# A fused attention, mixture of experts and recurrence kernel: two of four result tables read while the last experts run, and the last-slot store on another queue

## What is computed

```python
x = x + attention(layernorm(x))       # 16 heads of 16, 4 key groups, causal, soft cap
x = x + ffn(layernorm(x))
x = x + recurrence(layernorm(x))      # gates, then a scan over the rows
x = x + ffn(layernorm(x))

def ffn(x):                            # 64 experts, each row to 6 of them, 96 slots per expert
    topk_w, topk_i = top_k(masked softmax(x @ gate.T), 6)
    slot = expert * 96 + min(position among the expert's rows, 95)
    buf  = zeros(64 * 96, 256).at[slot].set(x[row])
    out  = (silu(buf @ Wg.T) * (buf @ Wu.T)) @ Wd.T       # per expert
    y    = sum over the 6 of out[slot] * topk_w
    return y + shared expert(x)
```

## Time and profile before

| | us |
|---|---|
| median of 3 runs | 1242.32 |
| the profiled execution's own time | 1246.5 |
| its span in the trace | 1244.3 |
| TensorE busy | 992.2 (80%) |
| ScalarE busy | 739.2 (59%) |
| DVE busy | 520.0 (42%) |
| POOL busy | 409.6 (33%) |
| attention, with the first routing of three and a half chunks | 0 to 600 |
| last half chunk, store of the last slots | 600 to 660 |
| experts, f = 0 | 660 to 821 |
| results, recurrence, second routing | 821 to 1050 |
| experts, f = 1 | 1050 to 1210 |
| results and stores | 1210 to 1244 |

### The profile page before, as it was taken

How to read it: one execution, slowest core, us unless ns; L and a number is a source line. 1 busy time by engine, 2 the same in 40 slices (tenths; PEclk the granted TensorE clock), 3 DMA queues, 4 the chain that set the end, 5 groups by cost and what they waited for, 6 DMA issues and landing times.

```text
span 1244.3 us, 20310 instructions
## 1 busy us (share of the span) xinstructions
PE 992.2 (80%) x7268; PEld 641.1 (52%) x7268; DVE 520.0 (42%) x1575; ACT 739.2 (59%) x982; POOL 409.6 (33%) x404
## 2 busy tenths in 40 slices
PE   5888787887888888877717999945787674999978
PEld 3543233332345455444316999932444443999966
DVE  7772711454212342430522333347876740333325
ACT  3588999999999999999102444414453300444420
POOL 0000000001230034055122556620288884566550
PEclk9999888988999999999667999966799876999987
DMA  9991000000110012000686999648132524999948
GB/s 352 394 392 69 1 1 1 18 1 17 49 55 29 1 49 74 10 14 3 196 221 172 289 290 288 144 135 267 62 125 108 174 56 116 267 296 283 264 56 329
DMA packets 94948, 176.21 MB, mean 142 GB/s; under 512 B 13134, under 2 KB 46895, under 8 KB 94848
## 3 DMA queue, kind: packets, MB, share of 16 engines
q1 hardware_dynamic: 57904, 130.02, 31.3%
q0 software_dynamic: 23616, 28.44, 10.8%
q10 hardware_dynamic: 13328, 16.45, 4.8%
HBM read 107.30 MB, written 83.72 MB: 154 GB/s over the span
## 4 chain that ended last, share of the span: by engine, by line
PE 28%; POOL 10%; DMA 4%; SPq 3%; issue 3%; DVE 2%; DVEq 1%; ACT 0%; POOLq 0%; ACTq 0%
PE PS L1465 14%; PE PS L1476 9%; POOL expert_in L335 7%; POOL pause L343 2%; PE PS L1452 2%; SPq L1261 2%; SPq L1262 1%; PE PS L1521 1%; PE PS L1505 1%; DMA expert_in<-lrow 1%; DMA spare_space<-expert_out 1%; DMA XE<-expert_in 1%; PE PS L1554 1%; DMA expert_out<-ob,yidx 1%; POOL expert_out L1351 0%
## 5 line engine op out<-in xcount | busy, mean ns | idle before, releaser
L335 POOL DMA_INDIRECT expert_in<-xp,didx x192 | 192.8, 1004 | 617.9 <-ACT PR L779 495.1
L774 ACT ACTIVATE PR<-PS 128x1024 f32<-128x1024 f32 (+3 forms) x312 | 277.1, 963 | 29.2 <-PE PS L643 13.7
L779 ACT ACTIVATE PR<-PR 128x2048 f32<-128x2048 f32 (+3 forms) x156 | 274.5, 1762 | 0.0
L1351 POOL DMA_INDIRECT expert_out<-ob,yidx x128 | 180.6, 1411 | 168.7 <-ACT ob L1663 125.8
L663 PE MATMUL PS<-PR,V 128*32 128x512 f32 (+3 forms) x768 | 96.0, 574 | 41.0 <-ACT PR L779 40.8
L1910 DVE SCALAR_TENSOR_TENSOR gta<-gth,PS 88x192 f32<-88x192 f32 x128 | 44.8, 350 | 193.1 <-ACT gth L1653 193.1
L643 PE MATMUL PS<-QT,KT 96*128 96x512 bf16 (+3 forms) x384 | 104.0, 364 | 12.2 <-ACT PR L774 9.4
L1653 ACT ACTIVATE gth<-PS 88x192 f32<-88x192 f32 x128 | 41.9, 327 | 107.1 <-PE PS L1465 107.1
L1663 ACT ACTIVATE ob<-PS,wslot 96x256 f32<-96x256 f32 x128 | 60.2, 470 | 61.8 <-PE PS L1476 59.5
L1465 PEld LDWEIGHTS PS<-XT,spare_space 128*88 128x88 f32 x960 | 92.0, 163 | 8.8 <-issue 2.6
L1465 PE MATMUL PS<-XT,spare_space 128*88 128x96 f32 x960 | 93.1, 253 | 2.1 <-ACT XT L1644 1.1
(11 more groups left out here) (271 smaller groups left out, 1535.0 us busy)
## 6 DMA issues: line engine op xcount, KB each, us to landing
spare_space<-in_wgu SPq DMA_DIRECT2D x60, 352.0 KB
expert_out<-zero SPq DMA_DIRECT2D x2, 8256.0 KB, 51.0
expert_in<-zero SPq DMA_DIRECT2D x2, 7776.0 KB, 39.6
XE<-expert_in ACTq DMA_DIRECT2D x32, 486.0 KB, 9.9
WGU<-in_wgu SPq DMA_DIRECT2D x44, 352.0 KB
spare_space<-expert_out SPq DMA_DIRECT2D x24, 512.0 KB, 6.2
spare_space<-in_wd SPq DMA_DIRECT2D x60, 176.0 KB
shared_space<-in_wgu SPq DMA_DIRECT2D x24, 352.0 KB
```

The lines of the kernel that those rows point to most:

```text
L335: pool.indirect_dma_start(out=buf_d[f], out_offset=bass.IndirectOffsetOnAxis(ap=didx[b][:, r, j:j + 1], axis=0), in_=xp[b][:, r, :], in_of ...
L774: act.activation(PR[:, n % 3, 2 * pr:2 * pr + 2, cols(v, s):CW], PS[:, S0 + 2 * pr:S0 + 2 * pr + 2, cols(v, s):CW], ACT.Tanh, scale=1.0 / ...
L779: act.activation(PR[:, n % 3, :, lo:CW], PR[:, n % 3, :, lo:CW], ACT.Exp, scale=SOFT_CAP).then_inc(exp_done, 1)
L1351: pool.indirect_dma_start(out=y_d[f], out_offset=bass.IndirectOffsetOnAxis(ap=yidx[:, n % 4, j:j + 1], axis=0), in_=ob[:, i % EU, :], in_o ...
```

## The change

- The store of the last slots is issued by ScalarE, which waits for the gathered rows itself, ahead of its waits for the dispatches.
- Experts 0 to 47 use the four tables as before. Experts 48 to 51 use tables 0, 1, 2, 0, and from 52 on only tables 0 and 1 in turn. `send(e)` waits for the expert that used its table last: 52 for 51, 54 for 52, and so on two apart.
- SP reads all of table 3 (when expert 47's rows have landed and its `down` is done) and all of table 2 (after expert 50's) as one DMA each, 16 rows of 1 KB to a partition, into two parts of `spare_space` whose weights have been used by then.
- DVE adds them to X, a chunk at a time: table 3 behind its products for experts 54 to 57, table 2 behind those for 59 to 62. The reads of the results also wait for these eight additions.
- After the experts two tables are read, 2 KB to a partition of a tile, and DVE and TensorE add two instead of four.
- `add_results(2)` moves behind `recur_inputs(0)`.

Cut to its core; `add_results`, the tiles by DVE in `combine_late`, the buffers `late_results` and the index table of `slot_meta` change in the same way, and f = 1 as f = 0:

```diff
--- before.py
+++ after.py
 NACC = 4
+LATE = 2
+TABLE_GROUPS = (0, 12, 13)
+
+def table_of(e):
+    return e % 4 if e < 48 else (e - 48) % 3 if e < 52 else e % 2
+
+def last_in_table(e, j):
+    return max([i for i in range(e) if table_of(i) == j], default=None)
...
-    ybase = np.broadcast_to(YBIG + np.arange(EH)[None, :] % NACC, (P, EH))
+    ybase = np.broadcast_to(YBIG + np.concatenate([tables[EH * h:EH * (h + 1)] for h in TABLE_GROUPS])[None, :], (P, EH * len(TABLE_GROUPS)))
...
-        GB = place_at(0, NACC).rearrange("p (r n) -> p r n", r=CT)
+        TA, TB = (place_at(NACC * i, NACC).rearrange("p (i n) -> p i n", i=NT) for i in range(2))
+        GB = place_at(0, LATE).rearrange("p (r n) -> p r n", r=CT)
...
-            def last_slots(f):
-                sp.wait_ge(last_rows, 16 * (f + 1))
-                sp.dma_start(buf_d[f].rearrange("(e s) c -> e s c", s=CAP)[:, CAP - 1, :], lrow[:]).then_inc(last_stored, 16)
...
+            def retired_tables(f):
+                for j, space, user in ((3, TA, 47), (2, TB, 50)):
+                    last = f * E + last_in_table(E, j)
+                    sp.wait_ge(y_sent[last % EU], 16 * (last // EU + 1))
+                    sp.wait_ge(down_psum, f * E + user + 1)
+                    sp.dma_start(space, y_d[f][0:NACC * T, :].rearrange("(i p k) c -> p i k c", p=P, k=NACC)[:, :, j, :]).then_inc(table_ld[3 - j], 16)
...
                         sp.wait_ge(y_sent[q], 16 * (E // EU) * (f + 1))
+                    sp.wait_ge(tables_added, 2 * NC * (f + 1))
                     sp.dma_start(O95[:], y_d[f][NACC * T:YROWS, :]).then_inc(o95_loaded, 16)
...
-                    sp.dma_start(results_tile, y_d[f][NACC * P * i:NACC * P * (i + 1), :].rearrange("(p k) c -> p (k c)", k=NACC))\
+                    sp.dma_start(results_tile.rearrange("p (k c) -> p k c", k=LATE),
+                                 y_d[f][NACC * P * i:NACC * P * (i + 1), :].rearrange("(p k) c -> p k c", k=NACC)[:, 0:LATE, :])\
...
-            last_slots(0)
             experts(0)
+            retired_tables(0)
...
-                if e >= NACC:
-                    pool.wait_ge(y_sent[(i - NACC) % EU], 16 * ((i - NACC) // EU + 1))
+                if last_in_table(e, table_of(e)) is not None:
+                    last = f * E + last_in_table(e, table_of(e))
+                    pool.wait_ge(y_sent[last % EU], 16 * (last // EU + 1))
...
-                        for j in range(NACC):
+                        for j in range(LATE):
                             last = pe.matmul(late_bank(i), const("ident"), late_results[c][:, r, j * C:(j + 1) * C], start=False,
...
+                act.wait_ge(last_rows, 16 * (f + 1))
+                act.dma_start(buf_d[f].rearrange("(e s) c -> e s c", s=CAP)[:, CAP - 1, :], lrow[:]).then_inc(last_stored, 16)
                 for b in range(NXP):
                     act.wait_ge(dispatched[b], 16 * CT * TOPK * chunks_in(b, NC * (f + 1)))
...
                     dve.drain()
+                    for j, space, first in ((0, TA, 54), (1, TB, 59)):
+                        if first <= e < first + NC:
+                            c = e - first
+                            dve.wait_ge(table_ld[j], 16 * (f + 1))
+                            xc = X[:, CT * c:CT * (c + 1), :]
+                            dve.tensor_tensor(xc, xc, space[:, CT * c:CT * (c + 1), :], ALU.add).then_inc(tables_added, 1)
...
-                tables = GB[:, r, :].rearrange("p (j n) -> p j n", j=NACC)
-                dve.tensor_tensor(tables[:, 0:2, :], tables[:, 0:2, :], tables[:, 2:4, :], ALU.add)
-                dve.drain()
-                dve.tensor_tensor(tables[:, 0, :], tables[:, 0, :], tables[:, 1, :], ALU.add)
+                dve.tensor_tensor(GB[:, r, 0:C], GB[:, r, 0:C], GB[:, r, C:2 * C], ALU.add)
...
             statistics(1, None)
-            add_results(2)
             for c in range(NC + 1):
...
                     recur_inputs(c)
+                if c == 0:
+                    add_results(2)
```

More of the change, by code:

```diff
@@ L73, in constants @@
     base = np.broadcast_to(BIG - CAP * e, (P, E))
-    lastv = YBIG - (NACC * T + p[:, None] - p[:, None] % NACC)
+    tables = np.array([table_of(i) for i in range(E)])
+    lastv = YBIG - (NACC * T + p[:, None] - np.resize(tables, P)[:, None])
     ycode = YBIG - NACC * (P * np.arange(NT)[None, :] + p[:, None])
-    ybase = np.broadcast_to(YBIG + np.arange(EH)[None, :] % NACC, (P, EH))
+    ybase = np.broadcast_to(YBIG + np.concatenate([tables[EH * h:EH * (h + 1)] for h in TABLE_GROUPS])[None, :], (P, EH * len(TABLE_GROUPS)))
     tok = P * np.arange(NT)[None, :] + p[:, None] + 1.0
@@ L183, in hybrid_kernel @@
         y_sent = [sem(f"y_sent{i}") for i in range(EU)]
+        table_ld, tables_added = [sem(f"table_loaded{i}") for i in range(2)], sem("tables_added")
         y_ld = [sem(f"y_loaded{i}") for i in range(CT)]
@@ L1219, in hybrid_kernel @@
         O95 = keep("O95", [E, C])
-        result_width = CT * NACC * C
+        result_width = CT * LATE * C
         late_results = [GB, WGU[:].rearrange("p e h m -> p (e h m)")[:, 0:result_width].rearrange("p (r n) -> p r n", r=CT),
                         WD_space[:, 0:result_width].rearrange("p (r n) -> p r n", r=CT),
-                        place_at(NACC, NACC).rearrange("p (r n) -> p r n", r=CT)]
+                        place_at(NACC, LATE).rearrange("p (r n) -> p r n", r=CT)]
         hc = keep("hc", [P, CH])
@@ L1316, in _ @@
             first_spare2(1)
-            last_slots(1)
             experts(1)
+            retired_tables(1)
             for c in range(NC):
@@ L1519, in combine_late @@
                         pe.wait_ge(late_ld[c][r], 16)
-                        for j in range(NACC):
+                        for j in range(LATE):
                             last = pe.matmul(late_bank(i), const("ident"), late_results[c][:, r, j * C:(j + 1) * C], start=False,
-                                             stop=(j == NACC - 1), skip_group_check=True)
+                                             stop=(j == LATE - 1), skip_group_check=True)
                     last.then_inc(rows_summed, 1)
@@ L1895, in slot_meta @@
                 w0 = C + EH * h
+                group = sum(h >= h0 for h0 in TABLE_GROUPS) - 1
                 dve.tensor_copy(wslot[:, s, :], flat[:, w0:w0 + (EH - 1) * (RW + 1) + 1:RW + 1])
-                dve.tensor_tensor(yidx[:, s, :], const("ybase")[0:CAP, :], XE[:, h % 2, :, VCOL], ALU.subtract)\
+                dve.tensor_tensor(yidx[:, s, :], const("ybase")[0:CAP, EH * group:EH * (group + 1)], XE[:, h % 2, :, VCOL], ALU.subtract)\
                    .then_inc(meta_ready, 1)
@@ L1926, in combine_late @@
                         dve.wait_ge(late_ld[c][r], 16)
-                        tables = rows[:, r, :].rearrange("p (j q n) -> p j q n", j=NACC // 2, q=2)
-                        dve.tensor_tensor(tables[:, :, 0, :], tables[:, :, 0, :], tables[:, :, 1, :], ALU.add)
-                    dve.drain()
-                    dve.tensor_tensor(rows[:, r0:r1, 0:C], rows[:, r0:r1, 0:C], rows[:, r0:r1, 2 * C:3 * C], ALU.add)
+                        dve.tensor_tensor(rows[:, r, 0:C], rows[:, r, 0:C], rows[:, r, C:2 * C], ALU.add)
                     dve.drain()
@@ L1969, in add_first_tile @@
                 dve.wait_ge(y_ld[r], 16)
-                tables = GB[:, r, :].rearrange("p (j n) -> p j n", j=NACC)
-                dve.tensor_tensor(tables[:, 0:2, :], tables[:, 0:2, :], tables[:, 2:4, :], ALU.add)
+                dve.tensor_tensor(GB[:, r, 0:C], GB[:, r, 0:C], GB[:, r, C:2 * C], ALU.add)
                 dve.drain()
-                dve.tensor_tensor(tables[:, 0, :], tables[:, 0, :], tables[:, 1, :], ALU.add)
-                dve.drain()
-                added = dve.tensor_tensor(X[:, r, :], X[:, r, :], tables[:, 0, :], ALU.add)
+                added = dve.tensor_tensor(X[:, r, :], X[:, r, :], GB[:, r, 0:C], ALU.add)
                 if r == CT - 1:
@@ L1982, in add_results @@
                     dve.wait_ge(y_ld[r], 16 * (c + 1))
-                    tables = GB[:, r, :].rearrange("p (j q n) -> p j q n", j=NACC // 2, q=2)
-                    dve.tensor_tensor(tables[:, :, 0, :], tables[:, :, 0, :], tables[:, :, 1, :], ALU.add)
-                dve.drain()
-                dve.tensor_tensor(GB[:, :, 0:C], GB[:, :, 0:C], GB[:, :, 2 * C:3 * C], ALU.add)
+                dve.tensor_tensor(GB[:, :, 0:C], GB[:, :, 0:C], GB[:, :, C:2 * C], ALU.add)
                 dve.drain()
```

## The result

| | before | after |
|---|---|---|
| median of 8 runs each, us | 1242.26 (1238.23 to 1243.95) | 1250.26 (1246.05 to 1257.96) |
| profiled execution, own time and span | 1246.5, 1244.3 | 1252.13, 1250.3 |
| mean granted clock in it (TensorE) | 0.901 | 0.896 |

**The change is slower: ratio 1.0069 [1.0046, 1.0093], 8.0 us.** Forecast were 1239 us and a range to 1250.

What follows compares the result with a forecast made beforehand. It took a chain of waits to bound the kernel: store and input load, TensorE in the stages, DVE then POOL between, TensorE's tail sums. -10.4 + 18.0 - 5.7 - 5.1 = -3.2 us gave 1239 against the median, range 1227 to 1250.

Steps and rivals of the forecast that it cites:

- Store of the last slots: Before the first expert stage: issued by ScalarE, it lands sooner and inputs are asked for at 640; 10.4 us gained.
- rival D: First stage: the moved store still takes 13.35 us among the loads, gain 4.3 instead of 10.4; 1245 us, chance 0.10.
- Tables in the stages: Both expert stages: DVE waits 6.5 us for table 3, clock 2, POOL 0.5; 18.0 us lost in all.
- later it catches up: Scatters from expert 52: two apart they fall behind 1 to 2 us each under table reads, then recover.
- Rival B: Expert stages: table wait 1 to 3 us, clock holds, scatters two apart cost 5 us each; 1231 us, chance 0.28.
- Between the stages: Between the expert stages: fewer DVE additions start the recurrence sooner, carried by POOL to the second stage; 5.7 us gained.
- The tail: Final table sums on TensorE: two tables instead of four; 7.8 us saved less 2.7 for the clock, 5.1 gained.
- But if the clock returns at the same moment: Tail: the third and fourth tile then run before the higher clock returns, which takes back 2.7 us.
- Rival C: Expert stages: slow table reads, 12 us of wait, a second wait at expert 59; 1252 us, chance 0.12.

Runs made afterwards that it cites:

- late additions: The change with DVE's additions behind experts 57 to 60 and 60 to 63 instead of 54 to 57 and 59 to 62: 1249.13 us, ratio 1.0078.
- three tables: The change with one table retired instead of two, its additions behind experts 58 to 61: 1232.38 us, ratio 0.9919; repeated, 1230.86 us, 0.9917.
- early additions: The change with one table retired instead of two, its additions behind experts 54 to 57: 1248.89 us, ratio 1.0064.

## Why the prediction was wrong

It said 1239 and gave 0.13 to slower. Three of its terms were mis-sized by more than 2 us: the store (10.4 forecast; some 6.7 against the median, below), the tail (5.1; measured 1.0), and the stages (18.0; measured 20.3). By its own steps:

- **Store of the last slots, -10.4.** Right for the trace it was made for (-11.7), wrong for the median. A row of after settles the rival D, ScalarE's store by line L1695:

```profile
DMA to landing us min/median/max: 2.0/4.2/6.5
```

  The larger is the first stage's, 6.5 us, where 13.35 and 11.6 to 11.8 were seen on SP's queue behind its weight loads. The Trainium skill (DMA: Bandwidth & Descriptors, "Issuing engines are not separate DMA queues") says that another issuer saves only the time of issuing; here the landing itself halved. The time of issuing was saved too: counted from the end of attention, ScalarE issued the store after 31.1 us, SP after 42.6. As an edit alone it measured 6.0 and 7.4: the term was sized from one execution whose store stretch, 56.0 us, was 3.7 longer than the 52.3 of other traces. The sum then also took off the 4.2 us by which that execution stood above the median. An estimate from these numbers is that the 3.7 us were counted twice, and 6.7 was the gain against the median.
- **Tables in the stages, +18.0.** The wait and most of the size were right (+9.7 and +10.6): the wait 6.2 and 6.5 for 6.5, and all else 3.5 and 4.1 for 2.5 (2 for the clock, 0.5 for POOL). Of that the last scatter's delay is 2.1 and 1.8, which the forecast had at nothing. The additions took 1.23 us in the change and at most 1.29 in any trace, and only POOL's scatters grew beside them (1.41 to 1.95 and 2.26 in the change, 2.37 with late additions). The Trainium skill (SBUF — State Buffer, "SBUF: two separate sides") has a lock that either side can lose; no addition of DVE was more than 0.06 us over its usual 1.23.
- **The step on the mechanism that failed here is "later it catches up. Behind a stall of 6.5 us it is hidden; if the stall were not there, the last scatter would come some 5 us late".** It does not catch up, and it is not hidden: 3.6 us were still there at the end of the stage. Without the stall the last scatter was 10.4 us behind the last scaling, 8.9 more than before. Rival B, 1231 at 0.28, rested on 5 us a stage; with 8.9 its own sum gives 1239, and with the 3.5 that were seen where no table was read 1228 (estimates).
- **Between the stages, -5.7.** The recurrence started 5.9 us sooner, counted from `O95` (39.2 before, 33.3 after); 860.32 - 854.5 in the forecast is 5.8, not 5.7. 1.5 us were lost again on TensorE ahead of the routing, in the gates' inputs (8.10 us before, 9.60 after, same 16 products), so POOL's first dispatch came 4.4 sooner. POOL had no gap after it and carried it on.
- **The tail, -5.1.** "But if the clock returns at the same moment" failed: it did not return at all, and the tail gave 1.0, under the lower bound of 2, which had been set for that very case. The forecast carried the moment over from before; with the same products in another order the clock did come back, so the work counts, and not the time alone. What in the work decides is not shown.
- **Attention, +2.8.** No step of the forecast, and no edit: it ended at 595.9 to 603.1 in the sixteen traces, whatever the kernel. A single profiled execution cannot tell a change of 3 us from this.

Against the medians the store's 3.7, the tail's 4.1, the stages' 2.3 and the 1.3 between them make 11.4 of the 11.2 us that were missed; each is from one trace or a few, so the agreement is in part luck.

The cost of the tables in the stages was nearly right (18.0 forecast, 20.3 in the trace), but of 10.8 us of credit for them 5.4 came, and the range, whose upper end of 1250 took in only half of C, was missed by 0.3. Rival C had nearly the right time (1252) by a wait that was not there: table 2 was never waited for. Nor do rows of 1 KB, 512 KB apart, read slowly here: from 790 to 794, when SP's queue with the two tables was the only one that moved data, it moved 363 GB/s.

## What to carry to other kernels

A chain of transfers that depend on each other at nearly the pace of the work cannot absorb a delay: compare landing plus issue over the distance with the pace, here 4.2 us against 4.38 for two, before reducing the number of buffers. When a wait is removed and nothing is gained, look for a second chain that was late beside it, and try both cures together: here late additions alone brought nothing, with three tables 18 us. And a saving on an engine whose clock depends on what it does is counted at both clocks.

## What was not expected of the hardware

- A small store of 64 rows landed in 6.4 to 7.3 us from ScalarE's queue (eight traces), and in 11.6 to 13.35 from SP's (four), behind the weights that SP had issued.
- TensorE's granted clock stayed at 0.50 through all of the change's tail, 1220 to 1247, without idle. With the same products in another order a row of the stretches shows it back:

```profile
1236.00:1244.00 8.00, 5.66 (x23) 4.49 (x21) 3.87 (x6) 0.00 (x0) 0.00 (x0) 0.90 0.37 126
```

- A read of 2.1 MB in 1 KB rows landed in 10.6 to 13.2 us in the change, and with one table in 15.0 to 15.6 with early additions, 11.2 to 13.8 with late ones and 14.6 to 15.7 in the repeat of those.
